# Gated cross-attention with an FP8 feed-forward: the second normalisation moved from ScalarE to VectorE, and all five instruction orders laid out anew

## What is computed

```
x1  = x + attn(layernorm(x), ctx, ctx)
out = x1 + ffn_fp8(layernorm(x1))        # layernorm(v) = (v - mean) / sqrt(var + 1e-5)
```

## Time and profile before

| | |
|---|---|
| median of 3 runs | 1749.72 us (1747.93 to 1753.19) |
| profiled execution, span | 1755.2 us |
| PE busy | 1600.4 us, 91% of the span |
| DVE busy | 1550.3 us, 88% |
| ACT busy | 1284.9 us, 73% |
| POOL busy | 1103.1 us, 63% |
| DMA engines, mean share | 0.83 between 400 and 1600 us |
| granted TensorE clock | 1.00 between 400 and 1600 us |

### The profile page before, as it was taken

One profiled execution on the slowest core, in us unless ns is written; L12 is line 12 of the kernel. 1 busy time (PEld: TensorE's weight loads), 2 busy tenths in 40 slices (PEclk: granted clock), 3 DMA queues, 4 the chain that ended last, 5 costly groups with the idle time before them and its releaser, 6 DMA issues.

```text
span 1755.2 us, 88770 instructions
## 1 busy us (share of the span) xinstructions
PE 1600.4 (91%) x36224; PEld 1193.1 (68%) x36224; DVE 1550.3 (88%) x4161; ACT 1284.9 (73%) x3137; POOL 1103.1 (63%) x1040
## 2 busy tenths in 40 slices
PE   3779999999999998999999999999999999999985
PEld 1567776777667676777776777776777777777762
DVE  6679988999888899998998989999999999998884
ACT  3657777777777777777777777777778777777653
POOL 1056666666566666666666666666667666666774
PEclk9889999999999999999999999999999999999996
DMA  4748978888878788788888788888888888887542
GB/s 165 206 150 222 247 214 214 231 232 216 235 218 225 218 213 232 217 232 229 226 221 232 214 226 230 225 239 214 225 241 225 226 231 240 218 223 216 166 134 84
DMA packets 329911, 376.11 MB, mean 214 GB/s; under 512 B 17056, under 2 KB 214688, under 8 KB 329504
## 3 DMA queue, kind: packets, MB, share of 16 engines
q1 hardware_dynamic: 329504, 370.40, 76.8%
HBM read 303.22 MB, written 67.11 MB: 211 GB/s over the span
## 4 chain that ended last, share of the span: by engine, by line
PE 61%; DVE 19%; issue 10%; DMA 7%; ACT 2%; POOL 1%; DVEq 0%; POOLq 0%; ACTq 0%
PE work L509 10%; PE y L548 9%; PE qk L477 9%; PE turn L392 7%; PE turn L403 5%; DMA o_sb<-in_x 4%; DVE dec L913 4%; PE work L489 3%; PE arg L446 3%; DMA out<-o_sb 3%; DVE bn L967 3%; DVE o_sb L1007 3%; PE y L532 2%; PE y L546 2%; PE work L521 2%
## 5 line engine op out<-in xcount | busy, mean ns | idle before, releaser
L1150 POOL TENSOR_TENSOR x<-x,h_r 128x512 f32<-128x512 f32 x256 | 269.6, 1053 | 268.9 <-DVE x L959 154.6
L1163 POOL TENSOR_TENSOR x<-x,w_out 128x512 f32<-128x512 f32 x256 | 358.1, 1399 | 20.1
L1168 POOL TENSOR_TENSOR x<-x,o_sb 128x512 f32<-128x512 f32 x256 | 321.1, 1275 | 33.7 <-DMA o_sb<-in_x 33.0
L509 PEld LDWEIGHTS work<-c_first,dec 128*64 128x64 f32 x4096 | 265.3, 138 | 72.1 <-issue 70.4
L509 PE MATMUL work<-c_first,dec 128*64 128x65 f32 x4096 | 290.8, 224 | 13.2 <-issue 6.4
L509 PE MATMUL work<-c_sb,dec 128*64 128x65 f32 x4096 | 292.7, 224 | 5.7 <-issue 5.7
L509 PEld LDWEIGHTS work<-c_sb,dec 128*64 128x64 f32 x4096 | 265.3, 138 | 6.4 <-issue 6.1
L548 PE MATMUL y<-w_ffn,zq 128*128 128x512 bf16 x1024 | 266.4, 383 | 0.0
L477 PE MATMUL qk<-qT,kT 64*64 64x128 f32 (+1 forms) x8192 | 235.8, 251 | 32.6 <-DVE dec L913 24.9
L614 ACT ACTIVATE dec<-arg 128x384 f32<-128x384 f32 x512 | 243.6, 476 | 27.9 <-PE arg L458 26.8
L1007 DVE SCALAR_TENSOR_TENSOR o_sb<-y,s_out,x 128x512 f32<-128x512 f32 x256 | 190.5, 744 | 73.1 <-PE y L548 72.3
(11 more groups left out here) (122 smaller groups left out, 4680.7 us busy)
## 6 DMA issues: line engine op xcount, KB each, us to landing
x_sb<-in_x SPq DMA_DIRECT2D x128, 512.0 KB, 5.1
kT<-in_keys SPq DMA_DIRECT2D x128, 512.0 KB, 6.7
c_sb<-in_ctx SPq DMA_DIRECT2D x256, 256.0 KB, 5.7
o_sb<-in_x SPq DMA_DIRECT2D x128, 512.0 KB, 4.5
out<-o_sb SPq DMA_DIRECT2D x128, 512.0 KB, 3.3
c_first<-in_ctx SPq DMA_DIRECT2D x256, 128.0 KB, 5.4
w_ffn<-in_L_ffn_kernel SPq DMA_DIRECT2D x1, 512.0 KB, 10.2
w_out<-in_L_xattn_out_w SPq DMA_DIRECT2D x1, 256.0 KB, 11.6
```

Of the source, the lines that this page charges most:

```text
L509: last = mm(work_ps[rows, u, c * W:(c + 1) * W], heads_dec[:, slot * Q:(slot + 1) * Q], src, start=True, stop=True)
L1150: pl.tensor_tensor(h, h, h_r[:, t * NH:(t + 1) * NH].unsqueeze(2).broadcast_to([P, NH, DH]), ALU.mult).then_inc(h_normed[t].sem, 1)
L1163: pl.tensor_tensor(h, h, w_out[:, :], ALU.mult).then_inc(h_scaled[t].sem, 1)
L1168: pl.tensor_tensor(x1[:, b.k % 2, t, :], x1[:, b.k % 2, t, :], o_sb[:, b.k % 2, t, :], ALU.add).then_inc(x1_set[t].sem, 1)
```

## The change

- `mix_scale` and its buffer nb2 are gone. `z_apply` is now a DVE `tensor_scalar` for each tile: (x1 - mean) x rstd, both scalars read by row from SBUF, output bfloat16. ACT has no `z_apply` any more.
- `mix_moments(b)` also waits for `z_set(b - 1)`, since `z_apply` now reads mv2; `m_rstds(b)` waits for `z_set(b - 1)` in place of the shift.
- The order lists of SP, PE, ACT, DVE and POOL are new. With the slot numbers read as names, PE has three moves: `arg` 3 now ahead of `ffn_turn`, `turn_round` 0 ahead of `scores` 1, `scan_rows` behind `ffn` 0. The other lists are stirred more.

The diff; of the removed order lists only the marks are left, since they stand above in the kernel before:

```diff
@@ -12,7 +12,7 @@
-FIRST, LAST = -10, 4
+FIRST, LAST = -11, 6
@@ -135,7 +135,6 @@
-        nb2 = sb("nb2", [P, T])
@@ -229,7 +228,7 @@
-        m_stats, m_moments, m_log, m_rstd, m_shift = (step(n) for n in ("m_stats", "m_moments", "m_log", "m_rstd", "m_shift"))
+        m_stats, m_moments, m_log, m_rstd = (step(n) for n in ("m_stats", "m_moments", "m_log", "m_rstd"))
@@ -353,18 +352,18 @@
             sp.wait_ge(pool_set, N_POOL_SET)
             def slot(m):
...
+                if live(m - 1):
+                    load_c(m - 1)
+                if live(m - 6):
+                    store(m - 6)
+                if live(m + 8):
+                    load_x(m + 8)
+                if live(m + 5):
+                    load_keys(m + 5)
+                if live(m - 4):
+                    load_own(m - 4)
+                if live(m - 1):
+                    load_first(m - 1)
             slots(slot)
             sp.wait_ge(stored, 16 * B)
@@ -550,6 +549,24 @@
                 last.then_inc(y_summed[t].sem, 1)
             def slot(m, wide_z):
+                if live(m + 2):
+                    arg(m + 2, 2)
+                if live(m + 1):
+                    within(m + 1, 1)
+                if live(m + 2):
+                    arg(m + 2, 3)
+                if live(m - 1):
+                    ffn_turn(m - 1)
+                if live(m + 9):
+                    turn_round(m + 9, 0)
+                if live(m + 2):
+                    scores(m + 2, 1)
+                if live(m - 1):
+                    ffn(m - 1, 0, wide_z)
+                if scans(m + 5):
+                    scan_rows(m + 5)
+                if live(m + 2):
+                    states(m + 2)
                 if live(m + 3):
                     arg(m + 3, 0)
                 if scans(m + 3):
@@ -728,18 +728,8 @@
             def m_rstds(b):
                 act.wait_ge(*m_log.of(b))
                 if b.follows(1):
-                    act.wait_ge(*m_shift.of(b - 1))
+                    act.wait_ge(*z_set.of(b - 1))
                 af(r2[:, :], log2[:, :], ACT.Exp, scale=-0.5).then_inc(m_rstd.sem, 1)
-
-            def z_apply(b, t):
-                if t == 0:
-                    act.wait_ge(*m_shift.of(b))
-                    if b.follows(1):
-                        act.wait_ge(*y_summed[1].of(b - 1))
-                done = af(z_bf[:, t, :], x1[:, b.k % 2, t, :], ACT.Identity, bias=nb2[:, t:t + 1],
-                          scale=r2[:, t:t + 1])
-                if t == T - 1:
-                    done.then_inc(z_set.sem, 1)
             def quantise(b):
                 act.wait_ge(*z_turned.of(b))
@@ -749,57 +739,53 @@
             def slot(m):
                 if live(m - 2):
...
+                    m_rstds(m - 2)
+                if live(m + 1):
+                    decay(m + 1, 2)
+                if live(m + 7):
+                    keep_gates(m + 7)
                 if live(m + 1):
                     decay(m + 1, 3)
+                if live(m - 2):
+                    quantise(m - 2)
+                if scans(m + 2):
+                    scan_exps(m + 2)
+                if live(m + 9):
+                    x_rstds(m + 9)
+                if live(m + 8):
+                    keep_turned(m + 8, 0)
                 if scans(m + 4):
                     scan_abs(m + 4)
+                if live(m + 1):
+                    keep_state(m + 1)
+                if scans(m + 4):
+                    scan_exp(m + 4)
                     scan_relu(m + 4)
...
+                    scan_log(m + 4)
                 if live(m):
                     normaliser_square(m)
...
                 if live(m + 2):
                     decay(m + 2, 0)
...
                 if live(m + 8):
                     keep_turned(m + 8, 1)
...
                 if live(m + 1):
                     keep_heads(m + 1)
                 if live(m + 9):
+                    norm_apply(m + 9, 0)
+                if live(m + 10):
+                    x_logs(m + 10)
+                if live(m):
+                    head_log(m)
+                if live(m + 2):
+                    decay(m + 2, 1)
+                if live(m + 9):
                     norm_apply(m + 9, 1)
+                if live(m):
+                    head_rstd(m)
+                if scans(m + 2):
+                    keep_facs(m + 2)
                 if live(m - 1):
                     m_logs(m - 1)
...
             slots(slot)
@@ -972,17 +958,19 @@
                 dve.wait_ge(*m_stats.of(b))
                 if b.follows(1):
                     dve.wait_ge(*m_log.of(b - 1))
+                    dve.wait_ge(*z_set.of(b - 1))
                 dve.sem_inc(dve_passed, 1)
                 ve.bn_aggr(mv2[:, 0, :], bn2[:, 0, :])
                 ve.bn_aggr(mv2[:, 1, :], bn2[:, 1, :]).then_inc(m_moments.sem, 1)
-            def mix_scale(b):
-                dve.wait_ge(*m_rstd.of(b))
-                if b.follows(1):
-                    dve.wait_ge(*z_set.of(b - 1))
-                for t in range(T):
-                    done = ts(nb2[:, t:t + 1], mv2[:, t, 0:1], r2[:, t:t + 1], -1.0, ALU.mult, ALU.mult)
-                done.then_inc(m_shift.sem, 1)
+            def z_apply(b, t):
+                if t == 0:
+                    dve.wait_ge(*m_rstd.of(b))
+                    if b.follows(1):
+                        dve.wait_ge(*y_summed[1].of(b - 1))
+                done = ts(z_bf[:, t, :], x1[:, b.k % 2, t, :], mv2[:, t, 0:1], r2[:, t:t + 1], ALU.subtract, ALU.mult)
+                if t == T - 1:
+                    done.then_inc(z_set.sem, 1)
             def quantise_wide(b):
                 pieces = zq_wide.rearrange("p c s -> p (c s)").rearrange("p (i n) -> p i n", i=WIDE_PIECES)
@@ -1058,58 +1046,59 @@
                     ffn_bias()
                 if m.k in range(FIRST + 4, FIRST + 4 + C):
                     ffn_weights(m.k - (FIRST + 4))
...
                 if live(m + 9):
                     norm_stats(m + 9, 1)
...
+                if scans(m + 2):
+                    scan_sums(m + 2)
                 if live(m - 4):
                     finish(m - 4, 1)
                 if live(m - 3):
+                    mix_stats(m - 3, 0)
+                if scans(m + 2):
+                    scan_a(m + 2)
+                if live(m - 2):
+                    head_centre(m - 2, 0)
+                if live(m - 3):
                     mix_stats(m - 3, 1)
...
+                if live(m - 1):
+                    carried(m - 1)
                 if live(m - 3):
                     mix_moments(m - 3)
+                if live(m):
+                    matrix(m, 0)
+                if live(m - 3):
+                    z_apply(m - 3, 0)
+                    z_apply(m - 3, 1)
+                if scans(m + 2):
+                    scan_max(m + 2)
                 if live(m - 2):
...
+                    head_centre(m - 2, 1)
+                if live(m - 1):
+                    keep_heads(m - 1)
+                if scans(m + 2):
+                    scan_exponents(m + 2)
                 if scans(m + 1):
...
+                    scan_rest(m + 1, 0)
+                if live(m - 1):
+                    normaliser(m - 1)
+                    head_stats(m - 1, 0)
+                    normaliser_clip(m - 1)
                 if live(m + 9):
                     norm_moments(m + 9)
...
                 if scans(m + 1):
                     scan_rest(m + 1, 1)
                 if live(m + 8):
                     norm_scale(m + 8)
...
                 if live(m + 10):
                     norm_stats(m + 10, 0)
...
                 if live(m - 3) and wide_z:
                     quantise_wide(m - 3)
                 if live(m - 3):
                     finish(m - 3, 0)
+                if live(m):
+                    matrix(m, 1)
+                if live(m - 1):
+                    head_stats(m - 1, 1)
             slots_by_range(dve, slot)
@@ -1169,19 +1158,18 @@
                                  ALU.add).then_inc(x1_set[t].sem, 1)
             def slot(m):
...
                 if live(m + 8):
...
                     scale_heads(m + 8, 0)
                     head_norm(m + 8, 1)
                     scale_heads(m + 8, 1)
+                    residual(m + 8, 0)
+                    residual(m + 8, 1)
                 if live(m + 9):
                     head_var(m + 9)
...
+                if live(m + 11):
+                    weigh_keys(m + 11)
+                if live(m + 9):
+                    head_norm(m + 9, 0)
             slots(slot)
```

More of the change, by code:

```diff
@@ L569, in slot @@
                     gates(m + 9)
[L570 to L586, removed]
             slots_by_range(pe, slot)
@@ L784, in slot @@
                 if live(m + 9):
+                    norm_apply(m + 9, 0)
[6 more added lines that the diff above has]
+                if live(m + 9):
                     norm_apply(m + 9, 1)
+                if live(m):
+                    head_rstd(m)
+                if scans(m + 2):
+                    keep_facs(m + 2)
```

(40 more changed lines are left out.)

39 lines of the change are left out of this document (removed).

## The result

The changed kernel takes **1870.12 us** (median of 4 runs, 1867.62 to 1875.13), the kernel before 1749.89 in the runs beside it: 1.0676 times as long, 95% interval 1.0641 to 1.0711. That is 120 us more. The forecast of 1728 us and its range were wrong; the first rival, worked out at 1869 us, is what came.

What follows compares the result with a forecast made beforehand. Bound: a balance of PE (12.0) and DVE (11.9 of 13.0 us), about 1 us a batch lost waiting for each other. Four batches sum to 51.5, 12.87 against 13.04: 22 us less, 1728 us; range 1690 to 1790.

Steps and rivals of the forecast that it cites:

- Where `z_apply` falls: On DVE: first half waits 0.5 us for POOL, second follows at once; 0.15 to 0.3 us a batch for PE.
- Rival 1: POOL gets between the two `z_apply` halves on DVE; second waits 1.28 us, 1.1 us more a batch, 1869 us; chance 0.17.
- The base of the sum: Four batches of the earlier trace, 51.2 us, become 51.5; 12.87 a batch, set against the average of 13.04.
- the third batch of the earlier trace: 13.33 us, less 1.0 for the buffer and 0.6 for `scan_a`, plus 0.5 for `z_apply` and 0.65 for the port: 12.9.
- Price of `z_apply`: On DVE: nearest row is the cast of the same shape, 426 ns; two in a row take 0.75 us of queue.
- DVE's room: DVE goes from 11.9 to 12.4 us a batch; the sum adds 0.5 in the third and fourth batches.
- The output buffer: `finish` 1 ahead of `mix_stats` 0 gives store, load and residual 1.25 us more; takes back 1.0 us in four batches.
- Rival 2: Fourth batch: rests late for PE's `arg` 0, each waiting for a whole POOL operation; 14.5 us, 1764 us total; chance 0.26.
- ACT's total: ACT loses `z_apply`, 1.6 of 10.0 us a batch; nobody waits for it; gives back part of `arg`'s 47.4 us.
- The sign that was named for rival 1: In the trace on DVE: second halves of `z_apply` of 1.5 us and more.

Runs made afterwards that it cites:

- Experiment 9: The changed kernel, with POOL's `head_norm` 0 and a scan's first `weigh_keys` waiting until `z_apply` of the batch before is done; 1781.17 us, 1.0199.
- experiment 11: The kernel before, with one more DVE statistics instruction of 512 columns (0.60 us, one input) behind `mix_scale`; 1789.87 us, 1.0232.
- experiment 8: The kernel before, with `finish` 1 put ahead of `mix_stats` 0 on DVE; 1749.92 us, 1.0006.
- experiment 2: The kernel before, with only `z_apply` moved from ACT to DVE in the place of `mix_scale`, all other order as before; 1952.44 us, 1.1140.

## Why the prediction was wrong, step by step

- **The step that failed** is the choice, in "Where `z_apply` falls", that "the second follows at once if DVE keeps the way", with 0.5 us of waiting ahead of the pair and 0.15 to 0.3 us a batch for PE. DVE doesn't keep the way. Its second operation is queued by the time at which it is asked for, and POOL's, asked for while the first runs, comes in between. The pair takes 1.75 us instead of 0.75 + 0.5: the second half waits in 74 of 128 batches and takes 1.40 us there, where the forecast had it follow at once. The wait of the first half isn't the one forecast either: as it was asked for, `head_norm` was mostly about to end and held it up in 3 batches, and the long ones stand behind `scale_heads`. Experiment 9 takes the meeting away and gives back 89 us.
- **Rival 1** had the mechanism and the time (1869), though partly by luck in its parts. It let the second half wait 1.28 us in most batches; it was 0.73 or 0.96 in three of five, and in most of the others the first half waited instead. What the rival left out, 0.26 us more at `head_centre` and 0.16 more work in the pair, made up for it. Its base was wrong too (next point). It was given 0.17. For it stood the order of asking in the earlier trace rows and my own times (3.8 before 4.0); against it only that DVE starts the next operation before the one ahead has ended, which no row connected with the way. By the Trainium skill ("SBUF — State Buffer", section "Who interferes with whom") whoever issues first has the shared pair for the whole instruction; this trace agrees, and shows that "the whole instruction" is meant of one instruction: the second half was issued 0.12 us behind POOL's and took 1.49 us instead of 0.53.
- **The base of the sum.** The changes that the sum lists add 0.3 us to the four batches of the earlier trace rows, from 51.2 to 51.5 us. The forecast set 51.5 against the average of 52.2, so its whole gain comes from the 1.0 us by which the average is longer. It put that 1.0 us down to the buffer, and yet took it off the third batch of the earlier trace rows as well. Like with like, the same terms give 0.3 / 4 x 128 = 10 us more, about 1760 us, and about 1790 without the buffer term; rival 1, with 1.1 us a batch more, would be near 1900. So rival 1's 1869 is right to 1 us by luck.
- **Price of `z_apply`**: 426 ns from the cast, measured 533, the pair 0.91 us of queue and not 0.75. Small, 0.16 x 128 = 20 us on an engine that bounds the kernel. That it stays below the 0.68 us of `head_centre` was right.
- **DVE's room**: the sum let 0.5 us a batch more work cost 0.5 in two of four batches, and the gains cover it. In experiment 11, 0.60 us of work cost 40 us, 0.31 a batch, more waiting at `head_centre` included. With no waiting at the pair the move and the new order cost 31 us (experiment 9).
- **The output buffer**: 1.0 us in four batches taken back, measured 0 for turning the two steps round (experiment 8), and in the changed kernel the wait grew to 139.5 us. That the average of four exceeded the four of the earlier trace rows by 1.0, and that the wait had that size, I took for a cause; no run shows that the one comes from the other.
- **Rival 2** was right that the rests become late for `arg` 0, wrong in size: 8.9 us in all, since the rests meet POOL less than before (926 ns).
- **Right**: ACT's total was nobody's bound; `arg`'s waits for it fell from 47.4 to 6.9 us, and no gain of it is seen. The sign that was named for rival 1, second halves of 1.5 us, is what stood in the trace.

The account in sum: 89 us go when DVE no longer meets POOL at the pair, and 31 us (1781 against 1750) are left for the added work, the new order and the guard together. No run separates these three; that work of this size can cost as much is suggested by experiment 11, 40 us for 0.60 us a batch, but a part of those 40 is waiting for POOL.

## What to carry to other kernels

A one-input VectorE operation in its fast form is cheap only where GpSimd isn't at work: count it as ending 0.28 us behind the GpSimd instruction that it meets (measured here for 512 columns, 0.53 us long by itself), for each of two in a row. Where such a meeting comes in every batch and GpSimd has time to spare, let GpSimd wait on a semaphore for the pair, or cut its instructions shorter; then look whether another wait took its place. A wait seen in the trace isn't yet worth its length, even if the chain runs through it: before you put it in a sum, make the one move that should shorten it and see whether the time follows (experiment 8). And compare a sum with the batches that it was built from, not with an average.

## What was not expected of the hardware

- The shared way is given by the time of asking from instruction to instruction, with no regard to which engine had it last: waits of 0.73 and 0.96 us (1.26 and 1.49 us against 0.53) for a difference in asking of 0.12 to 0.24 us; over all 74 it is 0.12 to 0.38 us. Statistics, with one input, of the same length and in the same place never waited (longest 0.56 us).
- `tensor_scalar` with two row scalars from SBUF, 512 columns from float32 to bfloat16, takes 533 ns; the cast of the same shape 426 to 428, and two-input operations of 512 columns 0.68 us.
- In experiment 2, where PE waits 1.8 us a batch for `carried`, the granted TensorE clock was 0.97 between 400 and 1600 us, where it is 1.00 before and after: less of the time was at the level of 2.4 GHz. Waits alone don't tell when that happens, since PE also waits in 126 batches of the changed kernel (1.2 us each) at 1.00. How much of the 1952 us the clock costs was not measured.
